# Graph network, two layers: one-hot stationary, gathered rows moving, sums node by feature in groups of 8 tiles

## The reference, cut to what matters

```python
# layer 0
t1    = x @ W1
msg   = (t1[src] + (x[src] * x[dst]) @ W2) / (sqrt(out_deg[src]) * sqrt(out_deg[dst]))[:, None]
agg   = segment_sum(msg, dst)
embed = leaky_relu(where(in_cnt > 0, t1 + agg, 0) + b0, 0.01)
x     = layernorm(x + embed / max(norm(embed), 1e-12))
# layer 1
out   = segment_sum((x @ W.T + b1)[src], dst) / (deg + 1)[:, None]
x     = layernorm(x + out)
```

## Time and profile before

| | us |
|---|---|
| median of the runs | 4266.98 |
| the profiled execution | 4292.12 |
| its span | 4290.4 |
| layer 0, first to last gather of the scaled table | 240.7 to 2247.7 |
| layer 1, first to last gather | 2270.6 to 4272.3 |
| busy: TensorE matmul / weight load | 3621.7 / 3168.4 |
| busy: GpSimd / VectorE / ScalarE | 3140.3 / 1600.2 / 381.6 |

### The profile page before, as it was taken

One profiled execution on the slowest core, in us unless ns is written; L12 is line 12 of the kernel. 1 busy time (PEld: TensorE's weight loads), 2 busy tenths in 40 slices (PEclk: granted clock), 3 DMA queues, 4 the chain that ended last, 5 costly groups with the idle time before them and its releaser, 6 DMA issues.

```text
span 4290.4 us, 60042 instructions
## 1 busy us (share of the span) xinstructions
PE 3621.7 (84%) x17483; PEld 3168.4 (74%) x17483; DVE 1600.2 (37%) x4104; ACT 381.6 (9%) x1359; POOL 3140.3 (73%) x3175
## 2 busy tenths in 40 slices
PE   6578888888888888888887888888888888888888
PEld 5477777877777777777776777777777777767776
DVE  9954444444444444444442222222222222222222
ACT  8800000000000000000000000000000000000000
POOL 2277777777777777777776777777777777777776
PEclk8755656666566656666565555555555555555555
DMA  5243333333333333343433344343343433434433
GB/s 164 87 129 115 111 115 113 112 115 110 115 110 116 111 114 115 110 115 109 116 109 98 112 117 117 112 116 113 116 117 112 117 114 114 118 111 117 117 113 104
DMA packets 236973, 489.92 MB, mean 114 GB/s; under 512 B 57537, under 2 KB 136916, under 8 KB 236948
## 3 DMA queue, kind: packets, MB, share of 16 engines
q0 software_dynamic: 150944, 409.95, 33.6%
q1 hardware_dynamic: 86004, 79.66, 5.8%
HBM read 450.84 MB, written 38.54 MB: 114 GB/s over the span
## 4 chain that ended last, share of the span: by engine, by line
POOL 69%; issue 25%; DVE 3%; PE 2%; POOLq 1%; DMA 0%; DVEq 0%; SPq 0%; ACT 0%; ACTq 0%
POOL ring L408 68%; DVE hot L598 2%; PE banks L1034 1%; POOL r_edge L416 1%; POOLq L444 0%; POOL ring L412 0%; PE banks L940 0%; POOLq L405 0%; PE banks L1013 0%; POOLq L406 0%; DVEq L590 0%; DVEq L640 0%; DMA ring<-in_dst 0%; PE banks L999 0%; DMA ring<-scaled_x,idx 0%
## 5 line engine op out<-in xcount | busy, mean ns | idle before, releaser
L1034 PE MATMUL banks<-dst_hot,ring 128*128 128x64 f32 x12544 | 2949.5, 395 | 562.5 <-DMA ring<-x,idx 250.8
L1034 PEld LDWEIGHTS banks<-dst_hot,ring 128*128 128x128 f32 x12544 | 2576.2, 294 | 938.3 <-DMA ring<-x,idx 377.0
L408 POOL DMA_INDIRECT ring<-x,idx x1563 | 1525.4, 976 | 499.2 <-issue 476.2
L408 POOL DMA_INDIRECT ring<-scaled_x,idx x1535 | 1539.4, 1003 | 467.9 <-issue 467.3
L743 DVE TENSOR_TENSOR big<-banks,big 128x128 f32 x784 | 228.7, 292 | 1936.8 <-PE banks L1034 1934.7
L715 DVE TENSOR_TENSOR dst_hot<-win_iota,dst_rel 128x256 f32<-128x256 f32 x787 | 337.0, 428 | 311.1 <-issue 310.9
L523 ACT COPY idx<-src_col 128x8 int32 (+1 forms) x392 | 77.5, 198 | 2875.4 <-PE banks L1034 2875.3
L940 PE MATMUL banks<-hot 128*128 128x98 bf16 x2848 | 210.7, 241 | 47.9 <-DVE hot L598 47.1
L940 PEld LDWEIGHTS banks<-hot 128*128 128x128 bf16 x2848 | 194.1, 120 | 67.6 <-DVE hot L598 44.8
L1013 PE MATMUL banks<-wt_s,a_t 128*128 128x256 f32 x392 | 179.0, 637 | 1.3 <-ACT a_t L537 1.3
L598 DVE TENSOR_TENSOR hot<-ring,count_to 128x2048 bf16<-128x2048 bf16 (+1 forms) x160 | 162.0, 1094 | 0.2
(11 more groups left out here) (118 smaller groups left out, 1043.4 us busy)
## 6 DMA issues: line engine op xcount, KB each, us to landing
ring<-x,idx POOLq DMA_INDIRECT x1563, 2.8
ring<-scaled_x,idx POOLq DMA_INDIRECT x1535, 2.8
x<-out_t SPq DMA_DIRECT2D x98, 128.0 KB
x_t<-x SPq DMA_DIRECT2D x98, 128.0 KB, 2.2
big<-in_x SPq DMA_DIRECT2D x1, 12416.0 KB
x_t<-in_x SPq DMA_DIRECT2D x97, 128.0 KB, 2.2
result<-out_t SPq DMA_DIRECT2D x97, 128.0 KB
scaled_x<-big SPq DMA_DIRECT2D x6, 1792.0 KB, 13.8
```

What stands on the lines that cost most here:

```text
L408: g.indirect_dma_start(ring[:, u, :], None, table[layer], bass.IndirectOffsetOnAxis(ap=idx[:, u:u + 1], axis=0)).then_inc(rows_in[u], 16)
L1034: last = nc.tensor.matmul(group_sum(k % 2)[:, f, :], ring[:, u, f * P:(f + 1) * P], dst_hot[:, k % HOTS, j, :], start=j == 0, stop=j == GT ...
```

## The change: what it does

The roles in the sum over edges are exchanged. The one-hot matrix (128 edges by the 128 nodes of a block) becomes the stationary operand and the gathered rows, with a column of ones behind them, the moving one: 257 columns. Sums stand with nodes on partitions, and the 257th column counts the edges of each node, so the counting of dst goes away. Groups have 8 tiles. A group's nodes are at most 128 wide but can lie across two blocks, so `add_group` adds the group's sums twice, to block b and to b+1, each times a 0/1 mask of the partitions. The node numbers 0 to 127 against which `group_hot` compares are read from PSUM (`lane_row`). The pair of node windows is mixed with nodes on partitions and turned afterwards: VectorE writes `halves`, TensorE transposes it, ScalarE copies it out of PSUM to `a_t`, and TensorE multiplies. GpSimd waits ahead of each quarter for `groups_done` as well, so that it begins group g only when groups up to g-2 are done. All 32 tiles of the first round are gathered raw.

```diff
-GT = 4
+GT = 8
-WIN = 64
+DW = D + 1
+PITCH = 264
-LAST_K = 2
+LAST_K = 1
+TURN_U = 20
+MIX_U = 24
+SUMS = 4
+LEAD = 2
-RAW = 7 * GT
+RAW = U
...
-            def gather_quarter(layer, i, q, end=U, begin=0):
+            def gather_quarter(layer, i, q, end=U):
 
                 g.wait_ge(idx_ready, (layer * ROUNDS + i) * 4 + q + 1)
+                g.wait_ge(groups_done, group_no(layer, i, q) - LEAD + 1)
                 g.sem_inc(gather_turn, 1)
...
-            for u in RAW_EARLY:
-                gather_raw(u)
-            g.wait_ge(r_made, 1)
-            for u in RAW_LATE[:RAW_FIRST]:
+            for u in range(RAW):
                 gather_raw(u)
             g.wait_ge(r_stored, 16)
-            for u in RAW_LATE[:RAW_FIRST] + RAW_EARLY:
-                gather_r(u, 0)
-            for u in RAW_LATE[RAW_FIRST:]:
-                gather_raw(u)
-            for u in RAW_LATE[RAW_FIRST:]:
-                gather_r(u, 1)
+            for u in range(RAW):
+                gather_r(u)
...
             def refill(layer, i, q):
 
-                act.wait_ge(tiles_done, (layer * ROUNDS + i) * U + q * QT + QT + U)
+                act.wait_ge(groups_done, group_no(layer, i, q) + 1)
...
+            nc.vector.tensor_copy(lane_row, count_to[:, :, 0])
             def group_hot(first_tile, buf, raw=False):
 
-                rel = dst_rel[:, bass.ds(first_tile, GT)].unsqueeze(2).to_broadcast([P, GT, WIN])
+                rel = dst_rel[:, bass.ds(first_tile, GT)].unsqueeze(2).to_broadcast([P, GT, P])
                 last = nc.vector.tensor_tensor(dst_hot[:, buf, :, :],
-                                               win_iota[:, :].unsqueeze(1).to_broadcast([P, GT, WIN]),
+                                               lane_row.unsqueeze(1).to_broadcast([P, GT, P]),
                                                rel, ALU.is_equal)
...
-                here = acc[:, :, bass.ds(base, WIN)]
-                nc.vector.tensor_tensor(here, group_sum(k % 2), here, ALU.add).then_inc(groups_added, 1)
+                for n in range(2):
+                    here = big[:, bass.ds((block + n) * DW, DW)]
+                    last = nc.vector.scalar_tensor_tensor(here, group_sum(k), here_mask[:, n, bass.ds(i * GR + k, 1)],
+                                                          here, ALU.mult, ALU.add)
+                last.then_inc(groups_added, 1)
...
-                v.wait_ge(x_turned, 2 * m + s + 1)
-                nc.vector.tensor_tensor(xa[s][:, :, :], turned[s][:, 0, :, :], sums, ALU.mult)
-                ordered()
-                nc.vector.tensor_tensor(sum_a[s][:, :, :], turned[s][:, 1, :, :], sums, ALU.add).then_inc(mixed, 1)
+                for s in range(2):
+                    v.wait_ge(x_in[s], 16 * (m + 1))
+                    nc.vector.scalar_tensor_tensor(halves[:, s, 0, :], x_t[s][:, :], root[:, bass.ds(2 * m + s, 1)],
+                                                   sums[:, s, 0:D], ALU.mult, ALU.add)
+                    nc.vector.tensor_tensor(halves[:, s, 1, :], x_t[s][:, :], sums[:, s, 0:D],
+                                            ALU.mult).then_inc(mixed, 1)
...
-                    if layer == 0 and k in (0, 3):
-                        half = k // 3
-                        hot_batch(SRC_BATCHES + 2 * i + half + 1, 2 * i + half + 1, 1 - half, 1)
-                    if layer == 0 and k % 4 == 1:
-                        add_hist(SRC_BATCHES + 2 * i + k // 4)
...
-                        for f in range(KF):
-                            last = nc.tensor.matmul(group_sum(k % 2)[:, f, :], ring[:, u, f * P:(f + 1) * P],
-                                                    dst_hot[:, k % HOTS, j, :], start=j == 0, stop=j == GT - 1)
-                        last.then_inc(tiles_done, 1)
+                        last = nc.tensor.matmul(group_sum(k), dst_hot[:, k % HOTS, u - k * GT, :], ring[:, u, 0:DW],
+                                                start=u == tiles[0], stop=u == tiles[-1])
+                        if u == tiles[-1]:
+                            last.then_inc(groups_done, 1)
+                        if finish and u == TURN_U - 1:
+                            turn_halves(layer, i - 1)
+                        if finish and u == MIX_U - 1:
+                            products(layer, i - 1)
```

More of the change, by code:

```diff
@@ L62 @@
 X_CHUNKS[0] = (0, X_CHUNKS[0][1])
-RAW = 7 * GT
-RAW_EARLY = [u for u in range(RAW) if 3 <= u < 13 or 20 <= u < 26]
-RAW_LATE = [u for u in range(RAW) if u not in RAW_EARLY]
-RAW_FIRST = 3
-FIRST_GROUPS = 3
+RAW = U
 DUMP = NPAD
@@ L134, in gnn @@
         root = sb("root", [P, NW])
-        r_diag = [sb(f"r_diag{n}", [P, P]) for n in range(2)]
-        columns = r_diag[0]
-        deg = sb("deg", [P, NW])
+        columns = sb("columns", [P, P])
         w1_s = sb("w1_s", [P, KF, D])
@@ L780, in finish_sums @@
                 else:
-                    nc.vector.tensor_scalar(pair[0], deg[:, two], 1.0, None, ALU.add)
+                    nc.vector.tensor_scalar(pair[0], sums[:, :, D], 1.0, None, ALU.add)
                     ordered()
@@ L872, in _ @@
                     if layer == 0:
-                        for s in range(2):
-                            mix(ROUNDS - 1, s, acc[:, :, (NW - 2 + s) * P:(NW - 1 + s) * P])
-                    for step in (finish_sums, moments, norm):
-                        step(layer, ROUNDS - 1)
+                        mix(ROUNDS - 1, acc[:, NW - 2:NW, :])
+                    finish_sums(layer, ROUNDS - 1, acc[:, NW - 2:NW, :])
+                    moments(layer, ROUNDS - 1)
+                    norm(layer, ROUNDS - 1)
             with v.Else():
@@ L978, in _ @@
             pe.wait_ge(weights_loaded, 96)
-            for o, half in enumerate(xa):
+            for o, half in enumerate(wl_s):
                 for k in range(KF):
@@ L1003, in products @@
-            def products(layer, m, s, taken):
-                if layer == 0:
-                    pe.wait_ge(mixed, 2 * m + 2 if s == 1 else 2 * m + 1)
-                    parts = [(xa[s][:, k, :], w2_s[:, k, :]) for k in range(KF)]
-                    parts += [(sum_a[s][:, k, :], w1_s[:, k, :]) for k in range(KF)]
-                else:
-                    pe.wait_ge(a_ready[s], taken + 1)
-                    parts = [(a_t[s][:, k, :], wt_s[:, k, :]) for k in range(KF)]
-                for k, (left, right) in enumerate(parts):
-                    last = nc.tensor.matmul(project[s], left, right, start=k == 0, stop=k == len(parts) - 1)
-                last.then_inc(projected, 1)
@@ L1016, in dst_hist, with turn_halves @@
-            def dst_hist(n, half):
-                pe.wait_ge(hist_added, n - SRC_BATCHES + 1)
-                hist_batch(n, half, True, True)
+            def turn_halves(layer, m):
+                for s in range(2):
+                    if layer == 0:
+                        pe.wait_ge(mixed, 2 * m + s + 1)
+                    elif s == 0:
+                        pe.wait_ge(sums_taken, m + 1)
+                    for h in range(2 if layer == 0 else 1):
+                        for k in range(KF):
+                            place = (h * KF + k) * P
+                            last = nc.tensor.transpose(turned[s][:, place:place + P], halves[:, s, h, k * P:(k + 1) * P],
+                                                       ident[:, :])
+                    last.then_inc(halves_turned, 1)
@@ new lines, in products @@
+            def products(layer, m):
+                weights = (w1_s, w2_s) if layer == 0 else (wt_s,)
+                for s in range(2):
+                    pe.wait_ge(a_ready[s], node_no(layer, m) + 1)
+                    parts = [(a_t[s][:, h, k, :], w[:, k, :]) for h, w in enumerate(weights) for k in range(KF)]
+                    for n, (left, right) in enumerate(parts):
+                        last = nc.tensor.matmul(project[s], left, right, start=n == 0, stop=n == len(parts) - 1)
+                    last.then_inc(projected, 1)
@@ L1037, in round_ @@
-                    if finish and layer == 0 and k == LAST_K:
-                        for s in range(2):
-                            turn_x(i - 1, s)
-                    if finish and k == LAST_K + 1:
-                        for s in range(2):
-                            products(layer, i - 1, s, i - 1)
+                    tiles = range(k * GT, min((k + 1) * GT, end))
+                    for u in tiles:
+                        rounds_before = layer * (ROUNDS if u < FINAL else ROUNDS - 1) + i
+                        pe.wait_ge(rows_in[u], 16 * (rounds_before + 1))
+                        last = nc.tensor.matmul(group_sum(k), dst_hot[:, k % HOTS, u - k * GT, :], ring[:, u, 0:DW],
[6 more added lines that the diff above has]
+                            products(layer, i - 1)
```

378 lines of the change are left out of this document (169 added, 209 removed).

## The result

The changed kernel takes 4176.39 us (median of 4 runs, 4174.81 to 4177.38), the kernel before beside it 4269.35 (4265.9 to 4276.45): ratio 0.978, 95% interval 0.9763 to 0.9797, 93 us faster. Forecast were 4197 us and a range of 4157 to 4258.

The account below looks back on a forecast made before the run. It took GpSimd's gathers, lengthened by VectorE's two-SBUF-input instructions, as the bound. Contention -81, start +1.5, layer-0 end +8 and layer-1 end +1.5 gave -70 us from 4267: 4197 us, range 4157 to 4258.

Parts of the forecast that it names:

- Gathers bound the kernel, TensorE doesn't: Both layers: GpSimd's gathers set the time at 1.254 us each undisturbed; TensorE, though 84% busy, isn't waited for.
- The lengthening comes from VectorE's operands in SBUF: Gathers, both layers: VectorE instructions with two SBUF inputs delay them at start or end, 125.1 us in all.
- L598, 98 pairs at 0.77 us, all of it under the second: Layer 0's digit one-hots for counting dst: each pair delays a gather by 0.77 us; removing them gives -75.5 us.
- The long one-hot and the adds are free from PSUM: New one-hot and two adds per group: with one input from PSUM they delay no gathers, cost 0.
- The rival that it would still hold them: The long one-hot still delays gathers: 0.43 us x 392 = 168 us, total 4365, slower; chance 5%.
- mix at 0.6 us a round, 29 us in all: Layer 0's four two-SBUF-input mixing instructions, 49 times, delay gathers by 0.6 us each time: 29 us.
- 10 us kept in layer 0 and 5 in layer 1: Gather delay remaining besides mix: 10 us in layer 0, 5 us from layer 1's finishing steps.
- Contention left: Gather delay by VectorE remaining after the change: 10 + 29 + 5 = 44 us of 125.1, so -81 us.
- Start +1.5 us: Start of layer 0: round 1's gathers begin at 243 to 253, taken as 248, against near 246.5 before: +1.5 us.
- Layer-0 end +8 us: Gap between the layers: turning after the mix, transposes, copies and undivided products add 8 us, from 5 to 11.
- Layer-1 end +1.5: End of layer 1: two transposes per window and their copies add 1.5 us, from 0 to 3.
- The wait for `LEAD` costs 0 in the layers, slack 7.4 us: GpSimd's wait per quarter: TensorE ends a round 5.7 us late, 7.4 are allowed, so cost 0.

Follow-up runs that it names:

- e5: Changed kernel, one-hot numbers in SBUF and each one-hot written by four instructions of 256 elements; other chip: 4907.59 us.
- e10: Changed kernel, one-hot numbers in SBUF, one-hot in four instructions of 256, run again on the other chip: 4951.96 us.
- e9: Changed kernel without the `groups_done` wait, b1 read from PSUM, products after tile 23 instead of 24; other chip: 4930.35 us.
- e7: Changed kernel plus a one-SBUF-input tensor_scalar (times 1.0, 1024 elements, in place) ahead of each one-hot; other chip: 4800.69 us.
- e1: Changed kernel with the one-hot L712 comparing against numbers in SBUF instead of PSUM, nothing else: 4279.06 us, ratio to before 1.0017.
- e3: Kernel before without counting dst in layer 0, and with the numbers of one-hot L715 in PSUM instead of SBUF: 4162.75 us, ratio 0.975.
- e6: Changed kernel with the four mix instructions issued twice in each round of layer 0; other chip: 4897.14 us.
- e4: Changed kernel without GpSimd's wait for `groups_done` ahead of each quarter: 4168.14 us, ratio to before 0.9762.
- e2: Kernel before without counting dst in layer 0 (deg set to 1, so output differs): 4228.85 us, ratio 0.9903.
- e11: Changed kernel without the `groups_done` wait, b1 from PSUM in L783, products after tile 23 instead of 24: 4165.31 us, ratio 0.9755.

## Why the prediction was right, and where it was off

- *Gathers bound the kernel, TensorE doesn't: right.* The gathers' period sets both layers in all kernels but e5 to e10, at granted clocks from 0.59 to 0.71. On the chip of those six something else adds hundreds of us (under e9), and e7, with the most lengthening of them, is the fastest.
- *The lengthening comes from VectorE's operands in SBUF: right, and shown* by e1 (+103 us for one operand) and e3 (-66 us for one operand on the other side). I had it as "two inputs"; e7 shows that one input can do it. The traces of before and after had it too: four gathers lose 0.4 us under the tensor_scalar L823 of before, 16 lose 1.5 us under L817 of after, the same step.
- *L598, 98 pairs at 0.77 us, all of it under the second: wrong in its parts.* Over layer 0 of before, 61 gathers start under the first L598 and lose 33.2 us, 44 under the second and lose 31.8, 65.0 us in all against my 75.5. One row can't give a mean: the gather of 0.95 us in the earlier trace rows had started 0.04 us ahead of the first L598, not under it. The other 17.7 us of layer 0 were L715 (9.4), L772 (4.2) and L807 (3.8), where I had 7.4 left. The error did the sum no harm, since L598 and nearly all of the rest went together.
- *The long one-hot and the adds are free from PSUM: right, but the earlier trace rows couldn't show it.* L753 and L755 there lie inside a gather, and L755 has 0.01 us to go when the next one starts; by the law two SBUF inputs would have cost nothing there either. Before had better rows: 24 gathers start with over 0.2 us of an L743 to go (PSUM and SBUF in) and lose nothing. The gathers under L712 keep 0.95 us. The rival that it would still hold them is the kernel e1, and there it would have cost 103 us; I had priced it at 168 by scaling the 0.77 of the earlier trace rows with the length, while the cost also needs a gather to start under it.
- *mix at 0.6 us a round, 29 us in all: the term that was mis-sized.* The 48 gathers that start under it lost 4.4 us, 0.09 each, and with twice the mixing 65 gathers lost 4.4 again (e6). I had scaled the price with the length of the whole run (1.8 us against 2.2), but a gather waits only for the one instruction under which it starts. With 0.13 us free and about 0.4 us from one instruction to the next, the average hit is estimated at (0.4 - 0.13)^2 / (2 x 0.4) = 0.09 us. Rows 4, 6 and 8 held that law already.
- *10 us kept in layer 0 and 5 in layer 1:* 0.2 without the mixing, and 9.0, of which 8.0 stand under one instruction, L783. Contention left was 13.6 us, not 44.
- *Start +1.5 us:* the first gather of round 1 came at 244.24, not 248, and before it had come at 246.71, so -2.5. TensorE worked through its second and third group at 3.5 us each, the rate of 2.4 GHz; I had taken the middle of both levels. The added `LEAD` wait costs 6.5 us here (e4), which the prediction had inside its 243 to 253 but not by name.
- *Layer-0 end +8 us:* +6.0, a gap of 28.96 against 22.93. *Layer-1 end +1.5:* -0.9.
- *The wait for `LEAD` costs 0 in the layers, slack 7.4 us: right.* In layer 0 the add of group g-2 starts 7.2 to 7.5 us ahead of the first gather of group g on average, by quarter. In layer 1 the add of group g-2 starts at least 6.6 us ahead (6.9 to 7.7 on average).
- *The profiled execution and the median.* The spans differ by 117 us, the medians by 93. Of the difference, 3 ns x 3094 = 9 us are in the base duration of a gather, 949 ns in the one execution and 946 in the other. That isn't the kernel: e2 and e3, of the code before, have 946, e11 and e5, of the code after, 949, and the profiled run of e11 is 4176.04 where its four others are 4164.74 to 4165.63. The other 15 us may be lengthening that this execution had beyond the median run; no trace of a median run shows it.
- *How near the forecast was:* partly luck. My terms are terms of the profiled spans, and there I forecast -70 and got -117, 30 of the 47 us from the contention. In the medians it is -70 against -93, because I carried the sum over unchanged, while the spans' difference is 24 us more than the medians'.

The spans add up: -111.2 lengthening, -9.3 base, -5.0 for four gathers less, +3.6 start, +6.0 gap, -0.9 end, together -116.8 against 4173.1 - 4290.4 = -117.3.

## What to carry to other kernels

Where GpSimd issues indirect DMAs back to back, look at the duration of these instructions before anything else: in these traces every tail above the sharp median was VectorE's doing, priced instruction by instruction, as the rest of the one that runs when GpSimd's starts, less some 0.13 us. So sum the loss over all gathers by the instruction they start under, rather than multiplying one row. Move one operand of that instruction to PSUM, or cut it into short pieces; both leave VectorE's amount of work as it is or raise it, and the kernel gets faster. And carry the sum to the median only after asking whether the profiled execution had the same base durations as the others.

## What the runs showed of the hardware that I had not expected

- One operand of one instruction form, 395 times, from PSUM to SBUF: +103 us in 4176 (e1).
- By the losses, a gather can be held at a point 0.13 us after its start, and at a second one, 0.83 us in; the second was seen with the tensor_scalar of e7 alone. A two-input L712 that begins inside a gather leaves it at 0.95 and is never longer itself (1.224 to 1.227 us at any start); the tensor_scalar is, 0.69 to 0.94.
- The base duration of a gather is 946 or 949 ns by the execution, worth 9 to 10 us.
- The same kernel (before) took 4272 us on one chip and 5044 to 5095 on another, with idle time on TensorE that nothing in the profile releases.
